# Later low parts of batch 1, rows rounded in two pieces in the last steps, an earlier block in the last expert, dummy products moved

## What is computed

```python
x = x + _L0_ffn_ref(_L0_cond_ref(x, itok_B_0_3, lora_A, lora_B, lang_embed),
                    expert_embeddings, first_linear, second_linear)
x = x + _L1_ffn_ref(_L1_cond_ref(x, W1, b1, v, itok_B_0_2), w1, b1, w2, b2)
# routing
    vals, idx = jax.lax.top_k(caw.T, expert_capacity)
    inter = jax.nn.relu(jnp.einsum('ech,eih->eci', tokens, first_linear))
    out = jnp.einsum('eci,ehi->ech', inter, second_linear) * vals[:, :, None]
# pooling
    attn_in = jnp.tanh(jnp.einsum('bsd,da->bsa', hidden, W1) + b1)
    scores = jnp.einsum('bsa,a->bs', attn_in, v)
    p = jax.nn.softmax(jnp.where(mask, scores[:, None, :], NEG_INF), axis=-1)
    pooled = jnp.einsum('bjl,bld->bjd', p, hidden) / cnt[..., None]
# feed-forward of layer 1
    xq = act_quant(rmsnorm(x))      # rows to 8 bits by their greatest value
    h = bitlinear(x, w1, b1); h = jax.nn.gelu(h); out = bitlinear(h, w2, b2)
```

## Time and profile before

| | |
|---|---|
| median of 3 runs | 734.63 us (733.26 to 735.54) |
| the profiled execution's own time | 732.48 us |
| its span in the trace | 730.6 us |
| busy: PE, DVE, ACT, POOL | 687.2, 474.9, 483.9, 390.2 us |

### The profile page before, as it was taken

How to read it: one execution, slowest core, us unless ns; L and a number is a source line. 1 busy time by engine, 2 the same in 40 slices (tenths; PEclk the granted TensorE clock), 3 DMA queues, 4 the chain that set the end, 5 groups by cost and what they waited for, 6 DMA issues and landing times.

```text
span 730.6 us, 9852 instructions
## 1 busy us (share of the span) xinstructions
PE 687.2 (94%) x3238; PEld 421.8 (58%) x3238; DVE 474.9 (65%) x866; ACT 483.9 (66%) x725; POOL 390.2 (53%) x427
## 2 busy tenths in 40 slices
PE   9899989999999999998788899999999999898997
PEld 6333667777777777783455455655556555453443
DVE  4288554545445545540356797887978879897895
ACT  1245436666367778871454979698796978968783
POOL 0202614563442615314867677777777767755554
PEclk9999999999999999999999999999999999999999
DMA  6999889998483948629302021131220111212122
GB/s 221 293 400 352 260 316 364 316 326 311 122 230 130 211 150 208 165 27 251 135 1 87 1 85 52 51 117 48 98 59 29 59 58 31 72 45 71 57 74 73
DMA packets 42627, 108.81 MB, mean 149 GB/s; under 512 B 5424, under 2 KB 7232, under 8 KB 39504
## 3 DMA queue, kind: packets, MB, share of 16 engines
q1 hardware_dynamic: 34352, 94.50, 36.7%
q0 software_dynamic: 7424, 13.06, 9.9%
q10 hardware_dynamic: 800, 0.61, 0.3%
HBM read 88.42 MB, written 28.13 MB: 160 GB/s over the span
## 4 chain that ended last, share of the span: by engine, by line
PE 48%; POOL 13%; issue 12%; ACT 7%; DVE 6%; DMA 3%; POOLq 0%; DVEq 0%; ACTq 0%; SPq 0%
PE ps L979 7%; PE ps L981 7%; PE ps L980 7%; PE ps L1416 6%; PE ps L1386 6%; PE ps L186 5%; POOL ht L1333 2%; POOL x_l L1237 2%; PE ps L971 2%; PE ps L970 2%; ACT h L1647 1%; ACT h L1640 1%; POOL xb L1341 1%; DMA choices<-token_choices,row_of_slot 1%; PE ps L1444 1%
## 5 line engine op out<-in xcount | busy, mean ns | idle before, releaser
L1386 PE MATMUL ps<-ff_q,qt 128*128 128x512 bf16 x512 | 124.2, 386 | 4.9 <-POOL qt L1295 3.3
L1416 PE MATMUL ps<-ff_q,ht 128*128 128x512 bf16 x512 | 120.8, 380 | 0.6 <-DVE res L1835 0.3
L797 POOL DMA_INDIRECT x_after_experts<-y,row_of_slot x32 | 51.6, 1612 | 130.0 <-DVE y L918 100.3
L979 PE MATMUL ps<-w_h,inner_l 128*128 128x512 f32 x256 | 102.0, 398 | 5.4 <-DVE inner_l L930 5.4
L1822 DVE SCALAR_TENSOR_TENSOR h<-ps,scale,bias 128x1024 f32<-128x1024 f32 x64 | 81.9, 1279 | 28.3 <-PE ps L1386 26.0
L981 PE MATMUL ps<-w_h,inner_h 128*128 128x512 f32 x256 | 100.1, 391 | 0.0
L980 PE MATMUL ps<-w_l,inner_h 128*128 128x512 f32 x256 | 100.0, 390 | 0.0
L865 ACT ACTIVATE inner_h<-ps 128x512 fp32r<-128x512 f32 x64 | 37.9, 592 | 70.5 <-PE ps L971 70.4
L1386 PEld LDWEIGHTS ps<-ff_q,qt 128*128 128x128 bf16 x512 | 48.0, 99 | 63.4 <-issue 8.2
L1827 DVE TENSOR_REDUCE h_mx<-h 128x1 f32<-128x1024 f32 x64 | 77.4, 1210 | 10.4 <-ACT h L1640 10.2
L1416 PEld LDWEIGHTS ps<-ff_q,ht 128*128 128x128 bf16 x512 | 48.8, 98 | 54.7 <-issue 1.8
(11 more groups left out here) (262 smaller groups left out, 1342.3 us busy)
## 6 DMA issues: line engine op xcount, KB each, us to landing
w_in_sb<-in_w_in_t SPq DMA_DIRECT2D x8, 2048.0 KB, 15.6
w_raw<-in_w_out_t SPq DMA_DIRECT2D x16, 1024.0 KB, 7.1
x_after_experts<-in_x SPq DMA_DIRECT2D x8, 1024.0 KB, 12.9
x_sum<-in_ff_t SPq DMA_DIRECT2D x8, 1024.0 KB, 9.8
raw<-in_ff_t SPq DMA_DIRECT2D x8, 1024.0 KB, 7.3
x<-x_after_experts SPq DMA_DIRECT2D x32, 256.0 KB, 2.9
out<-res SPq DMA_DIRECT2D x32, 256.0 KB, 3.1
x_sum<-x_after_experts SPq DMA_DIRECT2D x7, 1024.0 KB, 5.5
```

Source lines behind the costliest of these rows:

```text
L979: pe.matmul(ps[:, s, :], inner_l[:, r, c], w_h[:, k % RING, :], start=k == 0, stop=False)
L1386: m = pe.matmul(ps[:, ff_bank(t, half) + n, :], qt[:, t // TPB % 2, t % TPB, k, :], ff1_q[:, k, f * 512:(f + 1) * 512], start=k == 0, stop ...
L1416: mm = pe.matmul(ps[:, out_bank(t), :], ht[:, t % 2, k // 2, k % 2, :], ff2_q[:, k, :], start=k == 0, stop=k == KF - 1)
```

## The change

It makes these edits. In the first block, the dummy products are 10, 4 and 0 instead of 8, 2 and 4; all of `expand(1, 1)` comes ahead of `find(1, 0)`. In the last expert `inner_block(e, 7)` comes three output parts sooner, and the parts of tiles 0 and 1 come ahead of those of 2 and 3. In the prologue of the third block POOL makes `x_low(1, ...)` around `exp_args(1)` instead of ahead of `exp_args(0)`, and `x_high(2)`, `unpack_q(0)`, `exp_args(2)` come ahead of `x_low(2, ...)`; PE takes `side_sums(1)` ahead of two projections and `turn_q(0)` ahead of batch 1's pooling; ACT and DVE follow; batch 1's sums and batch 2's key scores get other banks, so that `first_matrix(0, 0)` needs `pool_cp` 6 instead of 7 copies, and some waits move. In steps after 20, `quantise` is cut in two pieces and `turn_q` comes one step later (j = 3), `keep_q` later in its step.

```diff
@@ -421,3 +421,3 @@
     pe.wait_ge(ones_ready, 1)
-    warm_up(pe, 8, FIND_BANK)
+    warm_up(pe, 10, FIND_BANK)
     pe.wait_ge(lora_in, 3 * DMA)
@@ -431,3 +431,3 @@
     m.then_inc(small_mm, 1)
-    warm_up(pe, 2, FIND_BANK)
+    warm_up(pe, 4, FIND_BANK)
     pe.wait_ge(small_cp, 1)
@@ -440,3 +440,2 @@
     pe.matmul(ps[0:W, COUNT_BANK, 0:BATCH], embed_score[:], lang_row[0:LANGS, :], start=True, stop=True).then_inc(small_mm, 1)
-    warm_up(pe, 4, FIND_BANK)
 
@@ -515,6 +514,5 @@
     expand(1, 0)
-    expand(1, 1, range(0, 2))
+    expand(1, 1)
     find(1, 0)
     find(1, 1)
-    expand(1, 1, range(2, KD))
     expand(2, 0)
@@ -1006,2 +1004,3 @@
         out_part(e, 4, 3).then_inc(k_mm, 1)
+        inner_block(e, 7)
         pe.wait_ge(in_l, KI * e + 6)
@@ -1010,4 +1009,2 @@
         out_part(e, 5, 1)
-        inner_block(e, 7)
-        out_part(e, 5, 2)
         pe.wait_ge(in_l, KI * e + 7)
@@ -1015,3 +1012,2 @@
         out_part(e, 6, 0)
-        out_part(e, 6, 1)
         pe.wait_ge(in_l, KI * e + 8)
@@ -1019,7 +1015,7 @@
         out_part(e, 7, 0)
+        out_part(e, 6, 1)
         out_part(e, 7, 1)
-        out_part(e, 6, 2)
-        out_part(e, 7, 2)
-        for k in (5, 6, 7):
-            out_part(e, k, 3)
+        for s in (2, 3):
+            for k in (5, 6, 7):
+                out_part(e, k, s)
 
@@ -1161,3 +1157,3 @@
             att_bank = lambda b: 0 if b == 1 else ATT_BANK
-            key_bank = lambda b: 0 if b == 1 else SMALL
+            key_bank = lambda b: {1: 0, 2: TRA}.get(b, SMALL)
 
@@ -1168,3 +1164,3 @@
 
-            num_bank = lambda b, j: (NUM, 0, 1, OUT)[j] if b < 2 else (NUM, NUM, ATT_BANK, NUM)[j]
+            num_bank = lambda b, j: ((NUM, 0, 1, OUT), (0, 1, NUM, OUT))[b][j] if b < 2 else (NUM, NUM, ATT_BANK, NUM)[j]
 
@@ -1299,6 +1295,6 @@
     pool.wait_ge(half_ready, 1)
-    for b in (0, 1):
-        x_high(b)
-        x_low(b, 0)
-        x_low(b, 1)
+    x_high(0)
+    x_low(0, 0)
+    x_low(0, 1)
+    x_high(1)
     pool.wait_ge(setup, 1)
@@ -1308,4 +1304,5 @@
     prob_low(0)
+    x_low(1, 0)
     exp_args(1)
-    x_high(2)
+    x_low(1, 1)
     split_side_keys(1)
@@ -1313,6 +1310,7 @@
     prob_low(1)
-    x_low(2, 0)
+    x_high(2)
     unpack_q(0)
-    x_low(2, 1)
     exp_args(2)
+    x_low(2, 0)
+    x_low(2, 1)
     def root(t):
@@ -1375,3 +1373,3 @@
         if t == 0 and half == 0:
-            pe.wait_ge(pool_cp, 2 * TPB - 1)
+            pe.wait_ge(pool_cp, TPB + 2)
         if t > LAST:
@@ -1430,2 +1428,4 @@
             pe.wait_ge(x_cp, KD * b + k - 1)
+        if b == 3 and k == 1:
+            pe.wait_ge(key_cp, 3)
         if k % 2 == 1 and t2 >= 0:
@@ -1450,3 +1450,3 @@
             pe.wait_ge(scanned, 1)
-        elif b >= 2:
+        elif b >= 3:
             pe.wait_ge(sum_l_cp, 2 * b)
@@ -1483,3 +1483,3 @@
             pe.wait_ge(pool_cp, TPB * b + min(j, 2))
-        if j == (1 if b >= 2 else 0) and b + 1 < BATCH:
+        if j == 1 and b != 1 and b + 1 < BATCH:
             pe.wait_ge(key_cp, b + 2)
@@ -1537,9 +1537,8 @@
     turn_x(2, 3, -1)
+    side_sums(1)
     project(2, 2)
     project(2, 3)
-    side_sums(1)
     score(2)
-    pool_block(1, 0)
     turn_q(0)
-    for j in range(1, TPB):
+    for j in range(TPB):
         pool_block(1, j)
@@ -1567,3 +1566,3 @@
             score(bx)
-        if j == 2 and inside(bq, BATCH):
+        if j == 2 and inside(bq, BATCH) and full(i):
             turn_q(bq)
@@ -1571,2 +1570,4 @@
             pool_block(bp, 2)
+        if j == 3 and inside(bq, BATCH) and not full(i):
+            turn_q(bq)
         if inside(t0, TILES):
@@ -1617,3 +1618,3 @@
 
-    def quantise(b):
+    def quantise(b, js=range(TPB)):
         act.wait_ge(to_q1_ready, b + 1)
@@ -1621,3 +1622,3 @@
             act.wait_ge(q_tr, b)
-        for j in range(TPB):
+        for j in js:
             act.activation(q8[:, j, :], pool_sb[:, j, :], ACT.Copy, scale=to_q1[:, j:j + 1]).then_inc(q8_ready, 1)
@@ -1666,5 +1667,5 @@
     keep_sums(0)
+    exps(1)
     for j in range(TPB):
         square(0, j)
-    exps(1)
     keep_x(2, 2)
@@ -1672,4 +1673,4 @@
     prob_high(1)
-    attend(2)
     keep_sums(1)
+    attend(2)
     quantise(0)
@@ -1699,2 +1700,4 @@
             gelu_half(t0, 0)
+        if j == 2 and inside(bq, BATCH) and not full(i):
+            quantise(bq, range(0, 2))
         if j == 1 and inside(bx, BATCH):
@@ -1718,2 +1721,4 @@
             act.activation(h_junk[:], h[:, t0 % 2, :], ACT.Square, accum_out=h_sq[:, t0 % 2:t0 % 2 + 1]).then_inc(h_squared, 1)
+        if j == 2 and inside(bq, BATCH) and not full(i):
+            quantise(bq, range(2, TPB))
     unpack_last_half()
@@ -1862,10 +1867,9 @@
         keep_pool(0, j)
-    greatest(0)
     norms(0)
+    greatest(0)
     sums_low(1)
     keep_keys(2)
-    maxima(2)
-    keep_pool(1, 0)
     keep_q(0)
-    for j in range(1, TPB - 1):
+    maxima(2)
+    for j in range(TPB - 1):
         keep_pool(1, j)
@@ -1919,4 +1923,2 @@
                 keep_pool(bp, 1)
-            if j == 3 and inside(bq, BATCH):
-                keep_q(bq)
             if inside(t3 - 1, TILES) and not full(i - 1):
@@ -1927,2 +1929,4 @@
                 keep_h(t2)
+            if j == 3 and inside(bq, BATCH):
+                keep_q(bq)
             if inside(t1, TILES):
```

More of the change, by code:

```diff
@@ L1313, in _ @@
                     prob_low(1)
+                    x_high(2)
+                    unpack_q(0)
+                    exp_args(2)
                     x_low(2, 0)
-                    unpack_q(0)
                     x_low(2, 1)
-                    exp_args(2)
                     def root(t):
@@ L1672, in _ @@
                     prob_high(1)
+                    keep_sums(1)
                     attend(2)
-                    keep_sums(1)
                     quantise(0)
```

4 lines of the change are left out of this document (2 added, 2 removed).

## The result

The changed kernel: median 734.52 us of 20 executions (724.66 to 740.37), against 735.52 us of the kernel before in the same comparison: 1.0 us less by the medians, 1.7 us by the means, where the single executions scatter by 4.9 us (standard deviation) against 1.8 us before. The ratio of 0.9927 (95% interval 0.9904 to 0.9950), which would be 5.4 us, leaves out as slow every execution over 1.5% above its kernel's fastest, eight of these twenty (mean clocks 0.974 to 0.978) and none of the kernel before, so it flatters a change whose cost is the clock. I had predicted 724.0 us (720.8 to 729.0), 10.6 us less. The profiled execution took 731.40 us, its span is 729.6 us.

The account below looks back on a forecast made before the run. PE has 48% of the chain of waits; five seams decide the time: +0.15 - 2.0 - 0.6 - 5.9 - 2.3 = -10.65 us against the profiled 732.48, giving 721.8, as a median 724.0 us; range 720.8 to 729.0.

Parts of the forecast that it names:

- Start of the third block: Third block's prologue up to first_matrix(4, 0): exp_args(0) and what follows start sooner; -5.9 us, bounds -4.6 and -7.2.
- the rule on the shared SBUF interfaces: Third block's prologue: POOL's x_low(1) would hold up DVE's top of batch 1 if they overlapped; forecast no overlap, by 0.7 us.
- Rival A: Half-clock stretches at the seams are moved, not saved; 4.5 us less gain, 728.5 us; chance 0.22.
- E's 740: Rival in the repeating steps: waits ahead of score join, two clock falls a batch make it slower, 740 us; chance 0.03.
- Last expert: End of the last expert: first y and POOL's adding DMAs come sooner; -0.6 us, bounds -1.4 and 0.
- expand before find: First block, up to L963's turn: L186's records fill PE's waits, the block ends sooner; -2.0 us, bounds 0 and -2.3.
- Dummy products: First block: moved dummies delay L436 by 1.36 us, feats(0) starts later; +0.15 us, bounds -0.4 and +0.5.
- The last steps: Steps 22 to 28: step 26's wait and clock fall go, first_matrix(24, 0) is 0.95 later; -2.3 us, bounds -0.6 and -3.3.
- the fall of the lower bound: Last steps: the clock falls in PE's new wait for q in step 27, costing 1.7 us and leaving -0.6 us.

Follow-up runs that it names:

- a_mask: Changed kernel with the masks' load issued behind those of x instead of at the end of the experts; 727.26 us median, ratio 0.9926.
- a_best: Changed kernel with the masks' load moved behind x, two dummy products around score(2) and two ahead of first_matrix(24,0); 720.45 us median, ratio 0.9851.
- a_order: Changed kernel with pool_block(1,0) ahead of turn_q(0) on PE again, masks' load in its old place; ratio 0.9955.
- a_front2: a_best with three more dummy products between L440 and the first products of x; 721.90 us median, ratio 0.9864.
- b_tail: Kernel before with the last steps' change alone; ratio 0.9999 (0.9978 to 1.0021).
- a_again: Changed kernel run once more, unaltered, for a second trace; 734.05 us median, ratio 0.9971.
- a_third: Changed kernel run once more, unaltered, beside the later versions on one chip; 729.95 us median, ratio 0.9955.

## Why the prediction was wrong

Two steps failed. The pooling products behind `turn_q(0)`, which I ran at full clock in my shifting, ran at half clock for 6.8 to 13.7 us; and the 2 us won ahead of the first expert were given back around it. Two smaller ones are the last expert's end and the wait in step 24.

**Start of the third block** (-5.9 us predicted). The shifts were right: `top` of batch 1 took 0.69 us behind `x_low(1, 0)`, the rule on the shared SBUF interfaces had nothing to act on; `side_sums(0)` ran at full clock; `score(2)` came 3.7 us sooner behind `turn_x(0, 0)`, 5.4 in `a_mask` and `a_best`, which lack the fall at 346 us, where I had 4.9. (`side_sums(0)` alone I had 4.4 us sooner at its end, though 3.1 + 3.44 - 2.3 is 4.2.) The step that failed is the one after: "`first_matrix(0, 0)` ... at 385.9". I priced PE's waits one by one and asked of each whether the clock would fall; I did not ask what stood between them. A wait of 0.78 us, the small products of `score(2)`, a wait of 0.70 us and eight transposes followed each other, where a pooling block had stood between. The length of a wait alone does not decide it: PE had waited 1.78 us ahead of `side_sums(1)` and kept its clock, and 1.61 us ahead of `score(2)` in the kernel before. PE was busy 3.79 of 5.10 us there and then stayed at half clock for 6.8 or 13.7 us of nearly unbroken pooling products. Of the five traces with that order and no dummies, four have the longer form (13.7 us), the first one the shorter. At full clock the seam is 6.3 us shorter; as they ran, D was 88.89 to 92.06 us against 90.51 to 92.15. The dummies show that the clock is what was missing; why it falls at this place stays open (`a_order`).

**Rival A** had the right mechanism and 0.22. Its size was off: "each half-clock stretch costs 1.3 to 1.7 us" holds (1.4), but it let falls only come back one for one. The kernel before had five stretches in its trace and one at its end; the changed one had, by the mean clocks of its twenty executions, 2 to 11 besides the end, 8 on average. (E's 740 is 742 by its own price, 724.0 + 2 x 9.)

The Trainium skill (TensorE: Matmul & The Clock Gate, "What's actually happening") says that the number of slow matmuls differs from run to run, since the gate's phase at the kernel's start is free. The executions here agree, with mean clocks of 0.995 to 0.974 for one program. The page speaks of the first matmuls; here later seams vary as well, as the 1.78 us wait of step 24 shows, behind which the clock fell in four traces and stayed up in two. I had read one trace of each fall as if it were the kernel's property.

**Last expert** (-0.6 us). The first adding DMA did come 0.41 us sooner behind block 60, and I wrote that "PE then stalls about 0.7 us and ends later by that" as if nobody waited for PE's end. SP does: it issues the masks' 480 KB at the block's end, and this now fell on the last adding DMA. C is 0.9 to 2.0 us longer than in the first trace, and 0.9 us longer in the mean of four traces than in the mean of five old ones (28.4 against 27.5); with the mask moved in both kernels it is 0.4 shorter. (The section on the change has `inner_block(e, 7)` three output parts sooner; it is two.)

**expand before find** (-2.0 us) was about right: from the second chosen rows (L471, L470) to L963 it is 21.93 us before and 19.75 us after in the first traces, 21.8 to 22.0 and 20.0 to 21.2 us in the others (1.5 us sooner in the mean of all), and by `inner_l` of block 4 it is 1.9 us where ACT has no unexplained wait. Where ACT stood idle, as in the first trace of the changed kernel and not in that of the kernel before, the first expert ran from the count to block 6 in 50.5 to 53.6 us against 46.8 to 48.7 us in the three old traces without the wait, so that A was 1.6 us longer there in spite of the front.

**Dummy products** (+0.15 us). I priced eight records at 0.23 us each from a row whose records start 0.21 us apart; in the first trace of the changed kernel eight take 1.16 us (from 6.19 us), 0.11 us apart. L436 came 0.2 us sooner there, not 1.36 later, and the first products of x started at 10.36 instead of 11.75 us. Part of that is luck: over all traces L436 starts at 6.3 to 7.5 us in the old order and 7.1 to 8.9 in the new, the first products at 10.5 to 11.8 and 10.2 to 12.0. What the term left out is the clock behind it. In six of nine traces of the new front the first products then ran slowly (five show 6.8 us at half clock there), which costs 2.3 us by the second chosen rows; in the old one the four dummies stood there, and one trace of five lost 1.4. `a_front2` shows that dummies ahead of them do not prevent it.

**The last steps** (-2.3 us). `b_tail` gave -2.2 with the clock up. The changed kernel's own traces have the fall of the lower bound, though not in the wait of step 27 where I had put it (1.33 us, clock up). It stands in step 24. I had the start of `first_matrix(24, 0)` right (+0.95, measured +1.05), but did not see that PE, which comes there early, waits 1.78 us for it, and asked nothing of its clock: the fall costs 1.4. That leaves -0.7, and 0.33 are lost at the end.

So the seams gave, in the profiled execution: A +1.6, B +0.2, C +0.9, D -3.3, F -0.8, G +0.3, together -1.1 of the -10.65 us. Of the 9.55 us that are missing, 3.4 lie in A, 2.6 in D, 1.8 in F and G, 1.5 in C and 0.2 in B. That trace has the shorter form of the fall; with the longer one, in `a_again` and `a_third`, D is only 0.4 to 0.5 us shorter than in the first trace of before, and the miss there is 5.4 to 5.5 us: in `a_third`, where ACT did not wait, nearly all of what is missing up to the last steps lies there and in C.
